# Graph convolution on one core: the running sums of a block enter the matmul accumulation through an identity product and are copied back by ScalarE

## The reference

```python
es, ev = h_s[edge_src], h_v[edge_src]            # 64 scalars, 32 vectors of 3
w = edge_query @ tp_weight                       # 64 -> 224 weights per edge
out0 = w0 * es * sh_s
out1 = (w1 * es)[:, :, None] * sh_v[:, None, :]
out2 = 2.0 ** (-0.5) * (w2a * sh_s)[:, :, None] * ev + 0.5 * w2b[:, :, None] * jnp.cross(ev, sh_v[:, None, :])
out3 = 3.0 ** (-0.5) * w3 * jnp.sum(ev * sh_v[:, None, :], axis=-1)
edge_x = jnp.concatenate([out0, out1.reshape(-1, 3 * MUL0), out2.reshape(-1, 3 * MUL1), out3], axis=1)
agg = jax.ops.segment_sum(edge_x, edge_dst, num_segments=n)
```

## Time and profile before

| | us |
|---|---|
| median of 3 runs | 9351.54 |
| lowest and highest | 9351.42, 9352.2 |
| the profiled execution: its own time | 9350.73 |
| its span, first to last instruction | 9349.0 |
| `conv_edges`: first and last add to `agg` start at | 6718.9, 9129.8 |

### The profile page before, as it was taken

How to read it: one execution, slowest core, us unless ns; L and a number is a source line. 1 busy time by engine, 2 the same in 40 slices (tenths; PEclk the granted TensorE clock), 3 DMA queues, 4 the chain that set the end, 5 groups by cost and what they waited for, 6 DMA issues and landing times. The chain is left out here.

```text
span 9349.0 us, 200867 instructions
## 1 busy us (share of the span) xinstructions
PE 8247.1 (88%) x48376; PEld 6585.1 (70%) x48376; DVE 8021.4 (86%) x21707; ACT 5330.8 (57%) x17719; POOL 5808.5 (62%) x5949
## 2 busy tenths in 40 slices
PE   5999999999999999999999947775688888888885
PEld 2788888888888888888888836663355555555555
DVE  3899999999999999999999865554599999999993
ACT  1566666666666666666666611111377777777771
POOL 0776666666666666666666347770277777777760
PEclk5999999999999999999999979995699999999995
DMA  1443333333333334343333336660233333333330
GB/s 64 107 106 104 103 104 103 104 103 104 102 104 102 104 102 104 102 105 102 105 102 104 85 101 177 177 179 13 52 91 89 89 89 89 89 89 89 88 80 17
DMA packets 932683, 916.70 MB, mean 98 GB/s; under 512 B 370528, under 2 KB 734688, under 8 KB 931744
## 3 DMA queue, kind: packets, MB, share of 16 engines
q1 hardware_dynamic: 690208, 498.68, 19.4%
q0 software_dynamic: 241920, 413.20, 18.1%
HBM read 762.86 MB, written 148.44 MB: 97 GB/s over the span
## 5 line engine op out<-in xcount | busy, mean ns | idle before, releaser
L464 POOL DMA_INDIRECT ae_gsrc<-tab_src,ae_idx x1616 | 1641.9, 1016 | 1281.1 <-DVE ae_msg L583 567.0
L1096 POOL DMA_INDIRECT ce_node<-tab_conv,ce_idx x1808 | 1708.4, 945 | 1059.9 <-issue 645.5
L467 POOL DMA_INDIRECT ae_gdst<-tab_dst,ae_idx x1616 | 1819.6, 1126 | 538.6 <-issue 538.6
L1186 PE MATMUL psum<-ce_prod,ce_plain 128*128 128x384 f32 x3616 | 1540.5, 508 | 337.7 <-DVE ce_prod L1159 275.7
L1171 ACT ACTIVATE ce_prod<-ce_raw,ce_y 128x64 f32<-128x64 f32 x5424 | 1464.4, 333 | 0.0
L596 PE MATMUL psum<-pack_sb,ae_rbfy 80*128 80x352 f32 x3232 | 1161.5, 461 | 21.1 <-DVE ae_minus L494 13.2
L616 PE MATMUL psum<-pack_sb,ae_first_t 128*128 128x288 f32 x3232 | 1118.4, 428 | 41.3 <-ACT ae_first_t L689 8.8
L1169 ACT ACTIVATE ce_prod<-ce_raw,ce_y 128x160 f32<-128x160 f32 x1808 | 752.8, 416 | 528.3 <-DVE ce_raw L1118 528.3
L1188 PEld LDWEIGHTS psum<-ce_prod,ce_plain 128*128 128x128 f32 x3616 | 688.0, 190 | 479.9 <-issue 2.1
L681 ACT ACTIVATE ae_mapped<-psum 128x192 f32<-128x192 f32 x808 | 267.6, 331 | 1287.0 <-PE psum L618 1287.0
L903 POOL TENSOR_TENSOR ag_exval<-ag_val,alpha 128x256 f32<-128x256 f32 (+1 forms) x904 | 638.3, 726 | 403.6 <-DMA ag_val<-h_dram 399.1
(11 more groups left out here) (169 smaller groups left out, 21056.3 us busy)
## 6 DMA issues: line engine op xcount, KB each, us to landing
ag_val<-h_dram SPq DMA_DIRECT2D x452, 320.0 KB, 3.2
h_dram<-ae_values SPq DMA_DIRECT2D x404, 320.0 KB
ae_rbf<-in_rbf SPq DMA_DIRECT2D x404, 160.0 KB
ce_query<-in_query SPq DMA_DIRECT2D x452, 128.0 KB
ae_y<-in_y SPq DMA_DIRECT2D x404, 128.0 KB
ce_node<-tab_conv,ce_idx POOLq DMA_INDIRECT x1808
ae_gsrc<-tab_src,ae_idx POOLq DMA_INDIRECT x1616
ae_gdst<-tab_dst,ae_idx POOLq DMA_INDIRECT x1616
```

The source lines that it names most:

```text
L464: pool.indirect_dma_start(gsrc[t.slot4][:, k, :], None, g["tab_src"], bass.IndirectOffsetOnAxis(ap=idx[t.pair][:, t.odd, k:k + 1], axis=0))\
L467: pool.indirect_dma_start(gdst[t.slot4][:, k, :], None, g["tab_dst"], bass.IndirectOffsetOnAxis(ap=idx[t.pair][:, t.odd, 4 + k:5 + k], axi ...
L1096: pool.indirect_dma_start(node[t.slot8][:, k, :], None, g["tab_conv"], bass.IndirectOffsetOnAxis(ap=idx[t.slot8][:, k:k + 1], axis=0))\
L1186: pe.matmul(b_a[t.slot], plain[t.slot4][:, k, :], prod[t.slot][:, k, 96:480], start=(k == 0), stop=False, skip_group_check=True)
```

## The change

DVE's add (L1129 to L1133) is gone. PE gets a register load of the block's number ahead of the sums, and behind the 8 products of a step one more: the 128x128 identity matrix as weights, the block's 384 running sums from `agg` as the moving operand, into the same accumulation. The bank then holds old sums plus new. It waits for `added` of the step before, since two steps in a row mostly have the same block. ACT gets, behind the scaling of step m, a register load and a copy of the bank of step m-1 into the block of `agg`, which gives the signal `added`.

```diff
                         ins.then_inc(outer_done, 1)
-                    t = m + -2
-                    if t.inside(STEPS):
-                        b = dve.value_load(g["step_b"][0:1, bass.ds(t.n, 1)], min_val=0, max_val=BLOCKS - 1)
-                        there = agg[:, bass.ds(b, 1), :].rearrange("p a c -> p (a c)")
-                        dve.wait_ge(summed, t.n + 1)
-                        wait(dve, added, t.n)
-                        dve.tensor_tensor(there, there, b_a[t.slot], ALU.add).then_inc(added, 1)
...
-                loop(dve, body, -1, STEPS + 2, STEPS)
+                loop(dve, body, -1, STEPS, STEPS)
...
+                    t = m + -1
+                    if t.inside(STEPS):
+                        b = act.value_load(g["step_b"][0:1, bass.ds(t.n, 1)], min_val=0, max_val=BLOCKS - 1)
+                        act.wait_ge(summed, t.n + 1)
+                        act.activation(agg[:, bass.ds(b, 1), :].rearrange("p a c -> p (a c)"), b_a[t.slot], ACT.Copy).then_inc(added, 1)
+                loop(act, body, 0, STEPS + 1, STEPS)
...
                         pe.wait_ge(prod_done, t.n + 1)
+                        b = pe.value_load(g["step_b"][0:1, bass.ds(t.n, 1)], min_val=0, max_val=BLOCKS - 1)
                         wait(pe, added, t.n - 1)
...
-                        ins.then_inc(summed, 1)
+                        wait(pe, added, t.n)
+                        pe.matmul(b_a[t.slot], w("ident"), agg[:, bass.ds(b, 1), :].rearrange("p a c -> p (a c)"), start=False, stop=True,
+                                  skip_group_check=True).then_inc(summed, 1)
```

More of the change, by code:

```diff
@@ L1159, in body @@
                         dve.tensor_tensor(out[:, :, 160:192], bank[:, :, 192:WW], dot[:, :, :], ALU.mult).then_inc(prod_done, 1)
-                loop(dve, body, -1, STEPS + 2, STEPS)
+                loop(dve, body, -1, STEPS, STEPS)
             @block.scalar
             def _(act):
[L1164 to L1174, removed]
+                def body(m):
+                    t = m
+                    if t.inside(STEPS):
+                        act.wait_ge(raw_done, t.n + 1)
+                        act.wait_ge(loaded[t.slot8], 48 * (t.eighth + 1))
+                        wait(act, summed, t.n - 1)
+                        for k in range(4):
+                            act.activation(prod[t.slot][:, k, 0:160], raw[t.slot][:, k, 0:160], ACT.Identity, scale=y[t.slot8][:, k, 0:1])
+                            for x in range(3):
+                                ins = act.activation(prod[t.slot][:, k, 192 + 96 * x:256 + 96 * x], raw[t.slot][:, k, 160:WW],
+                                                     ACT.Identity, scale=y[t.slot8][:, k, x + 1:x + 2])
+                        ins.then_inc(scaled, 1)
+                    t = m + -1
+                    if t.inside(STEPS):
+                        b = act.value_load(g["step_b"][0:1, bass.ds(t.n, 1)], min_val=0, max_val=BLOCKS - 1)
+                        act.wait_ge(summed, t.n + 1)
+                        act.activation(agg[:, bass.ds(b, 1), :].rearrange("p a c -> p (a c)"), b_a[t.slot], ACT.Copy).then_inc(added, 1)
+                loop(act, body, 0, STEPS + 1, STEPS)
             @block.tensor
@@ L1187, in body @@
                                       skip_group_check=True)
-                            ins = pe.matmul(b_a[t.slot][:, 96:384].rearrange("p (x c) -> p x c", x=3)[:, :, CS:96],
+                            pe.matmul(b_a[t.slot][:, 96:384].rearrange("p (x c) -> p x c", x=3)[:, :, CS:96],
                                             plain[t.slot4][:, k, :], prod[t.slot][:, k, 0:96].rearrange("p (x c) -> p x c", x=3),
-                                            start=False, stop=(k == 3), skip_group_check=True)
-                        ins.then_inc(summed, 1)
+                                            start=False, stop=False, skip_group_check=True)
+                        wait(pe, added, t.n)
+                        pe.matmul(b_a[t.slot], w("ident"), agg[:, bass.ds(b, 1), :].rearrange("p a c -> p (a c)"), start=False, stop=True,
+                                  skip_group_check=True).then_inc(summed, 1)
                     t = m + 1
```

## The result

The changed kernel takes **9586.02 us** (median of 4 runs, 9584.49 to 9588.15) against 9351.87 us for the kernel before beside it (9351.42 to 9352.68): a ratio of **1.0251, 95% interval 1.0239 to 1.0263**, 234 us slower. Forecast were 9630 and 279 us more. Its profiled execution has a span of 9582.7 us.

What follows compares the result with a forecast made beforehand. DVE and the loop through PE were taken as tied within 0.1 us; 5.67 + (0.25 + 0.60) + (4.65 + 0.67) + 0.09 = 11.93 us per two steps, +279 us, 9630 us; range 9485 to 9720, the forecast's own 9600 to 9665.

Steps and rivals of the forecast that it cites:

- The loop through PE: DVE's raw, prod, PE's sums, weights, raw two steps later in `conv_edges`: 10.71 us per two steps, tied with DVE's spacing.
- The register load: On PE behind all three waits, before the first sum: no cover, +0.52 to 0.70 us, 0.60 taken.
- rival B: Load or wait chain on PE costs about 1.2 us, twice what DVE shows: 9765 us; chance 0.10.
- The identity product: On PE between the sums and the weights, on the loop in full: +0.67 us.
- ACT's copy: 128x384 out of PSUM, about 0.5 us, placed in ACT's idle time behind the scaling, with no one waiting for it.
- the first term: From the start of DVE's raw to the end of `prod` and ACT's scaling: 5.67 us, instead of 5.68 before.
- the other three: To PE's first sum 0.85 us; sums, identity product and weights 5.32; weights' end to raw 0.09.
- rival A: PE's register load is hidden, only the identity product lengthens the loop: 5.665 us a step, 9494 us; chance 0.10.
- At most 0.1 us of the 0.47 comes back: On DVE without the add: the cross product must still wait for `outer_done`, so little of the add's spacing is regained.
- DVE's idle time: About 0.6 us per step before L1115, released by PE's weights L1201.
- Rival C: PE's work fits by busy time, 5.31 under 5.348 us a step: 9351 us, within 17; chance 0.08.
- Rival D: DVE sets the pace, the add's spacing comes back in full, PE's part is covered: 9139 us; chance 0.04.

## Why the prediction was right, and where its sizes were off

- **The loop through PE** was the reading that mattered, and it stands: load and product each cost time alone (90 and 93 us), although PE had idle time for either, moving the load or leaving out the product takes 177 and 154 us off the changed kernel, and with the weights ahead, which cuts the loop and covers the load, everything comes back (270).
- **The register load, 0.60 forecast**: 0.63 by the table, 0.88 against 0.25, and 0.67 from the load's start to the first sum. That 0.25 stays beside it was taken without a reason: with the scaling alone as the last signal it is 0.11 to 0.19, and the load's share is then 0.69 to 0.76. The sum of the two was forecast at 0.85 and is 0.88. The sequence is as long on PE as on DVE, as taken, and rival B (a dearer load) did not come. The median load takes 302 ns on PE and 305 on DVE. So the Trainium skill's floor of about 600 ns for a tensor_load (DMA: Bandwidth & Descriptors, Latency and other measured facts) fits the whole sequence, not the instruction.
- **The identity product, 0.67**: 5.34 - 4.65 = 0.69 by the table, and 0.68 between the changed kernel and the one without it (5.34 - 4.66). Right.
- **ACT's copy**: 0.47 to 0.49 us against "about 0.5". It was said that no one waits for it; PE's idle time is put down to it in the profile (92.6 us), but the copy that it names is that of the step before, for which only the identity product waits, some 4 us later. The last signal before the first sum is the scaling's, by 0.34 us in all of 250 steps.
- **The step that was mis-sized is the first term**, 5.67 forecast and 5.46 measured. Two steps were forecast 0.19 us too long: this term makes 0.21 of it, and the other three together 0.02 the other way. 0.19/2 x 452 = 43 us, of the 44 by which 9630 missed. I had read 0.78 us as what a 384-column instruction lasts on DVE. It lasts 0.55 when DVE has paused within the step, and the two kernels with DVE's add kept and only the load or only the product show it: their first term is 5.47. With L1118 done 0.23 earlier, ACT starts and ends its scaling earlier. With 9586 the time lies inside the wide range, which was drawn to hold rival A too, and 14 us below the forecast's own range of 9600 to 9665; this term is why.
- **"At most 0.1 us of the 0.47 comes back"** on DVE failed for the same reason. The cross product starts 0.59 us after the outer product (7510.18 less 7509.59) instead of 0.93, where 0.83 or more was forecast. So DVE gained 0.34 a step; its `prod` is done 5.12 us after raw starts, and this gain is lost because ACT's scaling ends at 5.46. The add left out of the kernel before shows what it was worth there: two steps fell by 0.42 us, 0.23 in the first term, 0.14 from there to the first sum, 0.04 before raw.
- **DVE's idle time**, 0.6 forecast, is 0.75: the step is 0.10 shorter than forecast, and DVE is busy only 865.16/170.4 = 5.08 us of it, where I had gone on with 5.35. Of the 0.79 us of idle time 0.75 lie before L1115.
- Rival C (no loop) is excluded by the product alone, rival A (hidden load) by the load alone. Rival D needed a cheap product and no loop; with the weights ahead the changed kernel is indeed faster than before, but by 35 us, since PE is then full. The rule of the Trainium skill that the prediction set beside rival D (VectorE: DVE Perf Modes, The DRAIN you can't avoid) is narrower than it was given there: the same section says that a next operation that is not held starts earlier, and with that the starts 0.46 us apart agree.

## What to carry to other kernels

An engine's idle time is room only if it is not spent waiting inside a loop of dependences: follow one step around (start of A, end of A, start of B, end of B, start of A again) and compare the sum with the step before putting anything there. A register load behind a data wait cost 0.66 to 0.76 us of the loop here, on an engine that had run dry, and ahead of the wait no cost of it could be seen. Work that the next stage of the loop waits for (here the weights, 1 us) belongs ahead of work that it doesn't wait for (the sums, 3.6 us and more): in the changed kernel that order gave 270 us, in the kernel before, where DVE's own work was as long as the loop, nothing. Moving work from a full engine to one nearly full pays in part only: with the weights ahead, every second step (9278 us) was better than all (9316) or none (9351).

## What the hardware showed that I had not expected

The duration of a DVE instruction in the trace depends on whether DVE has paused. In the kernel before, L1118 (384 columns) takes 549 ns at the start of the stage and more from step to step, up to about 780 ns some 40 steps later, while the distance between starts stays 0.46 us. Windows of 100 us at the stage's start and late in it:

```profile
L1118 DVE TENSOR_TENSOR ce_raw<-psum,ce_node x18: 549/592/651, 6703.7 to 6797.2; 128x384 f32<-128x384 f32 x18
```

```profile
L1118 DVE TENSOR_TENSOR ce_raw<-psum,ce_node x19: 759/783/794, 8499.7 to 8596.1; 128x384 f32<-128x384 f32 x19
```

With the loop cut and DVE never waiting it goes to 881 and stays there. In the changed kernel, in the one with only the load, and in the others above where DVE waits in each step or in every second, its median is 547 or 548. What lags behind the starts (and is caught up in a pause) the trace doesn't say. Its weight is real: ACT waits for L1118 and starts that much later, 0.23 us, and so the first term of the loop is longer by it. That the lag in the kernel before ended near 780 ns because there the loop through PE began to hold DVE back is my reading of 780 against 881; no run separates it.

Also unexpected: how long after the last of several signals PE starts depends on where its wait stands. In the kernel before, `prod_done` comes last in most steps and is waited for first, and the first sum starts 0.25 us later. With the scaling last it is 0.11 when its wait stands in the second semaphore instruction and 0.19 when it stands in the first of three waiting instructions. That is why 10.96 and 10.29 us were measured for two steps where 11.11 and 10.42 were expected. Whether another order of the waits would have gained as much was not tried.
